# State-space scans with a third buffer of input products and the gated output in the convolution's buffer

## The reference, cut to what matters

```python
xz = x @ in_w.T                      # x: layernorm of h
xh, z = split(xz)                    # 512 features each
xc = silu(conv_b + sum(xp[k : k + L] * conv_w[:, k] for k in range(4)))
dt, Bm, Cm = split(xc @ xproj_w.T)   # 16 states: Bm, Cm have 16 columns
delta = softplus(dt @ dt_w.T + dt_b)
h_t = exp(delta * A) * h_(t-1) + (delta * xc) * Bm    # for each of 16 states
y = sum over states of (h_t * Cm) + xc * D
out = (y * silu(z)) @ out_w.T
```

## Time and profile before

| | us |
|---|---|
| median of 3 runs | 5116.01 (5112.91 to 5116.14) |
| the profiled execution's own time | 5119.58 |
| its span, first to last instruction | 5117.9 |
| the 16 passes: first input_terms to the last addition to h | 1136.5 to 2881.3 of the span |
| mean granted TensorE clock | 0.935 |
| busy: TensorE, VectorE, ScalarE, GpSimd | 4445.0, 3499.4, 2189.7, 2460.3 |

### The profile page before, as it was taken

One profiled execution on the slowest core, in us unless ns is written; L12 is line 12 of the kernel. 1 busy time (PEld: TensorE's weight loads), 2 busy tenths in 40 slices (PEclk: granted clock), 3 DMA queues, 4 the chain that ended last, 5 costly groups with the idle time before them and its releaser, 6 DMA issues. The chain is left out here.

```text
span 5117.9 us, 65289 instructions
## 1 busy us (share of the span) xinstructions
PE 4445.0 (87%) x22600; PEld 2900.7 (57%) x22600; DVE 3499.4 (68%) x7168; ACT 2189.7 (43%) x4132; POOL 2460.3 (48%) x1575
## 2 busy tenths in 40 slices
PE   7888599948888888888888799997898899999999
PEld 4555487623333333333333345796344799999998
DVE  4664222248988989889898574311896788888885
ACT  3555011125555555555555454333664233333332
POOL 3442400059999999999999441000122133222332
PEclk8998799969999999999999799998999899999999
DMA  2002213332222222222222100374000100000000
GB/s 73 1 1 97 79 52 109 100 99 70 70 70 70 68 68 70 69 70 70 69 70 70 39 1 7 132 263 159 1 1 18 71 5 3 5 5 5 5 5 5
DMA packets 153112, 287.22 MB, mean 56 GB/s; under 512 B 24441, under 2 KB 135024, under 8 KB 144206
## 3 DMA queue, kind: packets, MB, share of 16 engines
q1 hardware_dynamic: 144926, 263.59, 15.7%
q0 software_dynamic: 6656, 14.04, 0.9%
q10 hardware_dynamic: 1200, 5.42, 0.3%
HBM read 252.33 MB, written 33.42 MB: 56 GB/s over the span
## 5 line engine op out<-in xcount | busy, mean ns | idle before, releaser
L1734 PE MATMUL ssm_ps<-ssm_hc,net_ident 128*128 128x452 f32 x2048 | 950.8, 590 | 197.3 <-DVE ssm_hc L1990 105.4
L1916 POOL TENSOR_TENSOR ssm_dBu<-ssm_du,ssm_bc 128x904 f32<-128x904 f32 x512 | 1067.3, 2110 | 3.2 <-POOL ssm_du L1934 1.9
L1835 ACT ACTIVATE ssm_ps<-ssm_step,ssm_decay 128x448 f32<-128x448 f32 x1024 | 647.8, 636 | 651.1 <-DVE ssm_ps L1980 438.1
L1734 PEld LDWEIGHTS ssm_ps<-ssm_hc,net_ident 128*128 128x128 f32 x2048 | 387.9, 202 | 729.8 <-issue 341.3
L1980 DVE TENSOR_TENSOR_SCAN ssm_ps<-ssm_ps,ssm_dBu 128x452 f32<-128x452 f32 x512 | 565.2, 1104 | 132.9 <-POOL ssm_dBu L1916 46.0
L1980 DVE TENSOR_TENSOR_SCAN ssm_hs<-ssm_ps,ssm_dBu 128x452 f32<-128x452 f32 x512 | 551.4, 1077 | 40.2 <-ACT ssm_ps L1835 35.7
L1927 POOL TENSOR_TENSOR ssm_hc<-ssm_hs,ssm_bc 128x904 f32<-128x904 f32 x256 | 539.8, 2109 | 73.9 <-DVE ssm_hs L1980 73.8
L3170 POOL TENSOR_TENSOR peer_hid<-peer_hid,peer_weight 128x452 f32<-128x452 f32 x256 | 288.7, 1168 | 525.7 <-ACT peer_weight L3120 525.7
L3035 PE MATMUL peer_ps<-peer_xn,peer_down 128*128 128x226 f32 x2048 | 439.3, 361 | 0.0
L3101 PE MATMUL peer_ps<-peer_hid,peer_up 128*128 128x226 f32 x2048 | 398.8, 355 | 2.7 <-POOL peer_hid L3170 2.2
L3101 PEld LDWEIGHTS peer_ps<-peer_hid,peer_up 128*128 128x128 f32 x2048 | 388.2, 190 | 11.2 <-POOL peer_hid L3170 4.1
(11 more groups left out here) (425 smaller groups left out, 8000.9 us busy)
## 6 DMA issues: line engine op xcount, KB each, us to landing
ssm_bc<-ssm_rows SPq DMA_DIRECT2D x256, 452.0 KB, 3.6
l_ff_w<-in_l_ffn_w SPq DMA_DIRECT2D x64, 1024.0 KB, 6.7
moe_w_gu<-in_moe_gate_up SPq DMA_DIRECT2D x16, 704.0 KB
slots_in<-rt_zeros SPq DMA_DIRECT2D x17, 640.0 KB, 8.5
moe_rows_in<-slots_in SPq DMA_DIRECT2D x16, 512.0 KB
slots_out<-xp_rows_out SPq DMA_DIRECT2D x16, 512.0 KB
moe_w_dn<-in_moe_down SPq DMA_DIRECT2D x16, 384.0 KB
peer_down<-in_peer_down_t SPq DMA_DIRECT2D x1, 4096.0 KB, 16.3
```

The source lines that it names most:

```text
L1734: nc.tensor.matmul(Y_BANK[j][:, 0:GT], c["ident"][:, :], hc[:, q % 2, j, :], start=False, stop=(n == S - 1))\
L1835: nc.scalar.activation(rows(dA(i % 2))[:, :, lo:lo + N - 1], rows(step[hf.d][:, j, :])[:, :, lo:lo + N - 1], ACT.Exp, scale=decay[hf.d][:, ...
L1916: nc.gpsimd.tensor_tensor(dBu[:, q % 2, j:j + 2, :], du[hf.d][:, j:j + 2, :], bc[:, q % RING, 0:1, :].to_broadcast([P, 2, GT]), ALU.mult). ...
```

## The change

A third buffer of dBu: `AHEAD = 3`, and input_terms of state q waits for the scans of state q - 3. GpSimd's order is at each n: output_terms(n - 1), then input_terms(n + 2) twice; at n = 0 input_terms(1) twice and input_terms(2) twice. The input_terms of the next pass's state 0, blocks 0 and 1, move from n = 15 to n = 14. The gated output no longer has a buffer `yz`: it is written into `conv`, so ScalarE's first tap waits for the output projection and VectorE's gates wait for the SiLUs that read `conv`.

```diff
--- before.py
+++ after.py
@@ -1594,10 +1594,11 @@
         bc_rows = st.sbuf("bc_rows", [BC, GT])
         mag = norm.square
         bc = st.sbuf("bc", [P, RING, 2, GT])
-        dBu = st.sbuf("dBu", [P, 2, IB, GT])
+        AHEAD = 3
+        dBu = st.sbuf("dBu", [P, AHEAD, IB, GT])
         hs = st.sbuf("hs", [P, 2, 2, GT])
         hc = st.sbuf("hc", [P, 2, IB, GT])
-        yz = st.sbuf("yz", [P, IB, GT])
+        yz = conv
         landed = [st.sem(f"landed{i}") for i in range(RING)]
         names = ("w_loaded", "zeros", "expd", "decay_done", "through_done",
                  "x_mm", "z_mm", "conv_step", "z_raw", "xc_done", "z_done", "xp_done", "rows_done", "row_sent",
@@ -1850,6 +1851,8 @@
                         if hf.front and i in TAP:
                             m = TAP.index(i)
                             act.wait_ge(s["x_mm"], IB * hf.fronts + m + 1)
+                            if hf.out_cols is not None:
+                                act.wait_ge(s["o_mm"], DK * (hf.outs + 1))
                             nc.scalar.activation(conv[:, m, :], XZ[:, 0:GT], ACT.Identity, bias=conv_b[f][:, m:m + 1],
                                                  scale=conv_w[f][:, m, TAPS - 1:TAPS]).then_inc(s["conv_step"], 1)
                         if hf.front and i in Z_RAW:
@@ -1907,13 +1910,13 @@
 
                         q = S * hf.r + n
                         pool.wait_ge(landed[q % RING], 16 * (q // RING + 1))
-                        if q >= 2:
-                            pool.wait_ge(s["scan_done"], IB * (q - 2) + AT[j + 1] + 1)
+                        if q >= AHEAD:
+                            pool.wait_ge(s["scan_done"], IB * (q - AHEAD) + AT[j + 1] + 1)
                         if q == 0:
                             pool.wait_ge(mixed_done, B)
                         if n == 0 and hf.fronts:
                             pool.wait_ge(s["du_done"], 2 * (hf.fronts - 1) + j // 2 + 1)
-                        nc.gpsimd.tensor_tensor(dBu[:, q % 2, j:j + 2, :], du[hf.d][:, j:j + 2, :],
+                        nc.gpsimd.tensor_tensor(dBu[:, q % AHEAD, j:j + 2, :], du[hf.d][:, j:j + 2, :],
                                                 bc[:, q % RING, 0:1, :].to_broadcast([P, 2, GT]), ALU.mult).then_inc(s["dbu_done"], 1)
 
                     def output_terms(hf, n):
@@ -1943,14 +1946,15 @@
                                 output_terms(hf, n - 1)
                             elif hf.carried is not None:
                                 output_terms(hf.carried, S - 1)
-                            if hf.rec and n + 1 < S:
-                                input_terms(hf, n + 1, 0)
-                                input_terms(hf, n + 1, 2)
+                            for ahead in (1, 2) if n == 0 else (2,):
+                                if hf.rec and n + ahead < S:
+                                    input_terms(hf, n + ahead, 0)
+                                    input_terms(hf, n + ahead, 2)
                             if n == S - 3 and hf.front:
                                 step_input(hf, 0)
+                            if n == S - 2 and hf.after:
+                                input_terms(halves[k + 1], 0, 0)
                             if n == S - 1:
-                                if hf.after:
-                                    input_terms(halves[k + 1], 0, 0)
                                 if hf.front:
                                     step_input(hf, 2)
                                 if hf.after:
@@ -1977,7 +1981,7 @@
                             state = hs[:, q % 2, j, :]
                             if q >= 2:
                                 dve.wait_ge(s["hc_pool"], q - 1)
-                        nc.vector.tensor_tensor_scan(flow(state, hf.d), flow(dA(i % 2), hf.d), flow(dBu[:, q % 2, j, :], hf.d),
+                        nc.vector.tensor_tensor_scan(flow(state, hf.d), flow(dA(i % 2), hf.d), flow(dBu[:, q % AHEAD, j, :], hf.d),
                                                      0.0, ALU.mult, ALU.add).then_inc(s["scan_done"], 1)
 
                     def output_term(hf, n, j):
@@ -2014,6 +2018,7 @@
                                 dve.wait_ge(s["z_done"], IB * hf.r)
                             if hf.outs:
                                 dve.wait_ge(s["o_mm"], DK * hf.outs)
+                            dve.wait_ge(s["xc_done"], IB * hf.fronts)
                             nc.vector.tensor_tensor(yz[:, j, :], Y_BANK[j][:, 0:GT], z[f][:, j, :], ALU.mult).then_inc(s["yz_done"], 1)
                         if hf.out_cols is not None and i in RES:
                             m = RES.index(i)
```

## The result

| | before | changed |
|---|---|---|
| median, us | 5114.54 (15 runs) | 5130.64 (15 runs) |
| lowest to highest, us | 5104.19 to 5119.0 | 5115.72 to 5145.36 |
| the profiled execution: own time, span | 5119.58, 5117.9 | 5120.27, 5118.6 |

The ratio is 1.0032, with a 95% interval of 1.0022 to 1.0042: the changed kernel is slower by 11 to 21 us, and its runs lie further apart. The predicted 5129 us was 13 us over the median known then.

A forecast was written before the change was run, and what follows sets the result against it. VectorE's own chain was taken as the bound: +26.9 us (pass starts and last pass) and -13.5 us (boundaries) made +13 on 5116.0, so 5129 us. Range 5102 to 5157 us with rivals, 5111 to 5137 for the forecast itself.

The forecast's parts named there:

- The bound: Inside the passes: VectorE's own chain bounds; it can get back at most 50.4 us, not GpSimd's 74.
- The boundary, -1.5 us each: Between passes: GpSimd is free earlier for du, saving 1.5 us at nine of 15 boundaries, -13.5 us.
- the six boundaries with a late decay: Pass ends where slot 62's decay comes 1.19 us late: nothing gained; bounds 0 and 0.65 us each, 4 us together.
- The start, first taps at E + 28.5: Pass start, E being the second scan's start: later out(0) delays TensorE's chain and VectorE's first tap; 0.4 to 2.2 us per pass.
- The last pass, +1.7 us: Last pass: GpSimd never waits, VectorE follows it, and scan (15, 2) comes 1.7 us later.
- The rest at nothing: Shared conv buffer's two new waits, instruction counts and row transfers cost nothing; the full clock is kept.
- rival D: Row transfer for state n + 2 holds back its input product: +48 us, 5177 us; chance 0.04.
- The sum: Whole kernel: 26.9 - 13.5 = +13 us on 5116.0, so 5129 us; chance 0.66.
- Rival A: The early delay is swallowed in VectorE's wait for ScalarE at slot 41; only -13.5 us is left, 5102.5 us; chance 0.13.
- Rival B: Two states of lead fill all GpSimd's idle time: -74 us, 5042 us; chance 0.03.
- Rival C: TensorE falls to 1.2 GHz behind its new idle time: 4 us in 7 forward passes, +28, 5157 us; chance 0.14.

The follow-up runs named there:

- experiment 4: The changed kernel with a third half of hs, so that no scan waits for output_terms: 5131.8 us, ratio 1.0031 to the kernel before.
- experiment 3: The changed kernel with GpSimd one input product ahead instead of two, from state 0 on: 5110.3 us, ratio 0.9984 to the kernel before.
- experiment 2: The changed kernel with the two extra input products made at state 8 instead of state 0: 5107.9 us, ratio 0.9984 to the kernel before.
- experiment 5: Kernel of experiment 2 with out(13) before the first du and no lead in the last pass: 5087.3 us, ratio 0.9950 to the kernel before.
- experiment 8: GpSimd's order of the kernel before, buffers of the changed one, out(13) before the first du: 5115.5 us, ratio 0.9996 to the kernel before.
- Experiment 1: The changed kernel's buffers and waits with GpSimd's order of the kernel before: 5119.9 us, ratio 1.0002 to the kernel before.
- experiment 9: The changed kernel with out(13) made before the first du: 5134.9 us, ratio 1.0045 to the kernel before.
- experiment 10: Kernel of experiment 9 with three unused TensorE products in the wait for out(0): 5122.0 us, ratio 1.0014 to the kernel before.
- experiment 6: Kernel of experiment 5 with the last du and its input products made block by block: 5060.4 us, ratio 0.9891 to the kernel before.
- experiment 7: The changed kernel with three unused TensorE products in the wait for out(0), forward and last passes: 5128.0 us, ratio 1.0025 to the kernel before.

## Why the prediction was right

**The bound.** The prediction took VectorE's chain for the bound and refused GpSimd's 74 us as a gain. Measured: GpSimd's wait for scans fell by 27 us and the time rose.

**The boundary, -1.5 us each.** Measured -1.4 (81.3 to 79.9 us from the first tap to the next second scan), in the form that was worked out. For the six boundaries with a late decay the prediction took 0, bounds 0 and 0.65. In the one where the decay stayed late, 0.8 came (pass 12 in the table); in the other five, where the clock was 1.00 after the change, 2.0 each: 10.7 us that were not counted. The other way round, two boundaries that had been good (10 and 14) had a late decay and gained nothing, and a third (8) gained 1.1. The sum over 15 is -20.5 us, not -13.5: this term was too small by 7 us, and that is the clock at the ends of passes, which the prediction held fixed. No run shows that the change causes the higher clock there.

**The start, first taps at E + 28.5.** Measured 28.6 in all middle passes but three. For the 25.2 us forecast for 15 passes, 31.1 came; the three forward passes at 30.1 add 4.5, the first pass cost 2.4 (taken 2.2), and the rest is 28.6 in place of 28.5. That the scans' wait does not carry it is shown by experiment 4, whose next wait is for TensorE's projection, that two instructions of lead are what it takes, by experiment 3, and that the place is the pass's start, by experiment 2.

**The last pass, +1.7 us.** Measured +1.8 at slot 62; experiment 5, which takes the lead out of the last pass, has slot 62 at E + 93.6 again. At the last addition to h the profiled pair hides it: E + 111.1 before, with the low clock shown above, and 110.3 after. In the traces without the lead in the last pass and without that low clock (experiments 3, 5 and 8) the addition ends at E + 108.5, so the 1.8 us are real.

**The rest at nothing.** Experiment 1: right. The row transfers never held a product back: no wait for a transfer stands before line 1919, so rival D did not come up.

**The sum.** 5130.6 us is the median of 15 runs for 5129 forecast, and 16 us over the kernel before for 13. The profiled pair has +12.4 us up to slot 62 of the last pass, +9.8 up to the last addition. That the sum came out this near is luck in part: the cost was 6 us larger than forecast and the gain 7 us larger, and the two cancel. Both are the clock for the most part. The sum gave every pass the clock that it had before, and three starts then had a lower one and five ends a higher. Rival A fell in experiment 2. Rival B did not come. Rival C was there inside the forecast: not 4 us in seven passes but 1.5 us in three. Experiments 9 and 10 show it larger, six first taps late by 9.2 us in sum, in a kernel that differs from the changed one by the place of one instruction. That runs of the changed kernel spread over 30 us fits a number of low passes that varies from run to run; one profile per kernel cannot show that, so it stays open.

**What the change could have been.** The gain at the end of a pass is real and the third buffer pays for it. The lead is better taken where GpSimd stands idle anyway (state 8), out(13) comes ahead of du so that TensorE's work does not hang on it, and the last step reaches the second scan by block. The kernel of experiment 6 has all three: 5060 us, 0.9891 (0.9876 to 0.9906), under both kernels.

## What to carry to other kernels

When an engine that serves two others gets further ahead for the one, ask what it now hands later to the other: the instructions moved to the front delay everything behind them by their own time, once per pass, until the engine next stands idle, so take the lead at that idle place. A wait that shows as new in the list of waits need not be the one that costs; take it away (experiment 4) before believing it. And compare the stretch that was changed, from a marker in it to a marker in it, not spans: here the spans agreed to 0.7 us while the changed part had lost 9.8 up to its last instruction, and 12.4 up to a marker some 16 us earlier.

## What the runs showed of the hardware

TensorE came back from 3.2 us without work with a granted clock of 0.59 in the next 4 us, and a pair of matmuls took 1.88 us there (third pass of the changed kernel). After 1.69 us without work (ninth pass) and after 0.70 us (experiment 7) it stayed at 1.00. The Trainium skill (TensorE: Matmul & The Clock Gate, Part 1) says that the array is throttled unless activity releases it; the rows agree. In experiments 9 and 10 useless matmuls put into the wait made a kernel faster: ratio 1.0045 without and 1.0014 with them, 8.1 us in the profiled pair.

GpSimd's products kept 2.06 us from start to start with an idle time of 2.6 us moved from one place to another, and a product of half the width took 1.14 us against 2.10. By that about 0.2 us of each are fixed (an estimate: 2 x 1.14 - 2.10).
